# A four-layer graph network on one core: a node pass with longer lags, an edge pass with four transpose buffers and a reordered VectorE

## The reference

```
ft = (feat @ W).reshape(n, 8, 32)
e = leaky_relu(einsum(ft, attn_l)[src] + einsum(ft, attn_r)[dst])
ex = exp(e - segment_max(e, dst)[dst]);  alpha = ex / segment_sum(ex, dst)[dst]
x = layernorm(x + elu(segment_sum(ft[src] * alpha, dst)))
h = (x @ W3.T).reshape(n, 4, 64)          # start of the fourth layer
```

## Time and profile before

| | us |
|---|---|
| median of 3 runs (lowest, highest) | 5583.04 (5579.09, 5586.88) |
| the profiled execution, its own time | 5618.38 |
| its span, first to last instruction | 5616.6 |
| busy PE, DVE, ACT, POOL | 4466.3, 3371.4, 1907.7, 3767.0 |
| edge pass of layer two, first POOL instruction to the barrier | 3246.9 to 3890.6 |
| node pass, from there to its barrier | 3890.6 to 4580.8 |

### The profile page before, as it was taken

The page is one execution under the profiler, slowest core; times in us unless marked ns, Lnnn a source line. Parts: engine busy times, 40 slices in busy tenths (PEclk is TensorE's granted clock), DMA queues, the critical chain, the costliest instruction groups (busy, mean ns, idle before and its releaser), DMA issues. The chain is left out here.

```text
span 5616.6 us, 68003 instructions
## 1 busy us (share of the span) xinstructions
PE 4466.3 (80%) x17208; PEld 2963.8 (53%) x17208; DVE 3371.4 (60%) x9357; ACT 1907.7 (34%) x3319; POOL 3767.0 (67%) x3395
## 2 busy tenths in 40 slices
PE   2477669999999999999999967774777656656765
PEld 1255435556666666666666656664666533322222
DVE  1255456566666666666666547676555548945655
ACT  0011135532222222222222244453444420026765
POOL 7488644445777777777777767774555568856674
PEclk7688889999999999999999988886888978878887
DMA  9999899987744334433334255655777756658886
GB/s 378 307 202 207 193 279 365 361 310 275 260 136 133 128 127 132 134 132 127 123 131 132 99 181 200 217 212 176 259 264 261 264 189 226 240 172 282 309 310 218
DMA packets 530526, 1214.70 MB, mean 216 GB/s; under 512 B 172297, under 2 KB 267697, under 8 KB 530370
## 3 DMA queue, kind: packets, MB, share of 16 engines
q1 hardware_dynamic: 344392, 963.16, 48.4%
q0 software_dynamic: 147728, 214.04, 14.3%
q10 hardware_dynamic: 38250, 35.85, 2.0%
HBM read 623.69 MB, written 721.15 MB: 239 GB/s over the span
## 5 line engine op out<-in xcount | busy, mean ns | idle before, releaser
L1123 PE MATMUL psum<-W2b,arena 128*128 128x256 f32 x3136 | 725.2, 379 | 0.0
L840 DVE TENSOR_SCALAR arena<-arena 128x256 f32<-128x256 f32 x784 | 476.9, 669 | 388.2 <-POOL arena L835 383.4
L1104 PE MATMUL psum<-arena,W1b 128*128 128x512 f32 x1568 | 699.1, 599 | 0.0
L1123 PEld LDWEIGHTS psum<-W2b,arena 128*128 128x128 f32 x3136 | 573.1, 190 | 66.3 <-issue 0.5
L1946 POOL DMA_INDIRECT hd_d<-arena,FL x392 | 382.2, 975 | 306.6 <-DVE arena L1992 185.2
L618 PE MATMUL psum<-arena,half 128*128 128x324 f32 x980 | 355.2, 528 | 284.0 <-ACT arena L409 156.6
L2092 POOL DMA_INDIRECT arena<-fin_d,FL x392 | 427.3, 1090 | 184.6 <-issue 118.0
L1012 ACT ACTIVATE arena<-psum,hbias 128x512 f32<-128x512 f32 x392 | 270.0, 689 | 804.2 <-PE psum L1104 794.7
L1104 PEld LDWEIGHTS psum<-arena,W1b 128*128 128x128 f32 x1568 | 289.8, 190 | 402.4 <-issue 402.4
L967 POOL DMA_INDIRECT xl_d<-arena,FL x392 | 389.0, 992 | 118.7 <-issue 116.4
L959 POOL DMA_INDIRECT xd_d<-arena,FL x360 | 378.6, 1052 | 99.5 <-issue 99.2
(11 more groups left out here) (291 smaller groups left out, 8926.4 us busy)
## 6 DMA issues: line engine op xcount, KB each, us to landing
arena<-in_x SPq DMA_DIRECT2D x194, 512.0 KB
x_d<-arena SPq DMA_DIRECT2D x194, 512.0 KB
tab<-zero SPq DMA_DIRECT2D x11, 5832.0 KB
arena<-x_d SPq DMA_DIRECT2D x105, 512.0 KB
h_d<-arena SPq DMA_DIRECT2D x97, 528.0 KB
arena<-h_d SPq DMA_DIRECT2D x97, 528.0 KB
h_d<-arena SPq DMA_DIRECT2D x98, 512.0 KB
arena<-h_d SPq DMA_DIRECT2D x98, 512.0 KB
```

The lines of the kernel that those rows point to most:

```text
L840: v.tensor_scalar(y[:, j, :], r[:, j, :], self.mv[:, j, 0:1], self.rs[:, j:j + 1], ALU.subtract, ALU.mult).then_inc(self.s["y"], 1)
L1104: last = pe.matmul(psum[:, HB[c], :], W1b[:, f, c * P:(c + 1) * P], x1T[:, f, :], start=False, stop=(f == FH - 1))
L1123: last = pe.matmul(outB(j), hid[:, c, j * P:(j + 1) * P], W2b[:, c, :], start=(c == 0), stop=(c == KH - 1))
```

## The change

In the edge pass there are 4 PSUM banks and 4 `xT` buffers for transposes in place of 2 (and 4 banks in place of 6 for products). PE transposes 3 chunks ahead of its products in place of 1, ACT copies out 2 ahead in place of 1. DVE's turn g becomes logits(g), finish(g-2), shares(g), chain(g) in one piece. POOL scatters 23 chunks behind in place of 25. The elu stands one chunk earlier in ACT's order, and in the join the last `finish` stands in DVE's list behind the first four operations of the join. In the node pass to_rows stands 6 turns behind in place of 4 and the store of hs 4 turns behind in place of 2; xT has 4 buffers, so that evac(k) waits for mm(k-4); and the stores of hs count on semaphores of their own (`gd`), so that normed waits for stores of y alone and to_rows for those of hs alone. What other phases count on is adapted.

```diff
@@ edge_pass2
-            F0, NF = 2, 6
+            NT, NF = 4, 4
...
-            LAG = 25
+            LAG = 23
-                return F0 + c % NF
+                return NT + c % NF
...
-                    wait(pe, r["ev"], c - 1)
+                    wait(pe, r["ev"], c - NT + 1)
-                tr(0)
+                for c in range(NT - 1):
+                    tr(c)
                 for c in range(C):
-                    if c + 1 < C:
-                        tr(c + 1)
+                    if c + NT - 1 < C:
+                        tr(c + NT - 1)
                     mm(c)
-                    wait(act, r["mm"], c - 1)
+                    wait(act, r["mm"], c - NT + 1)
-                    if c + 1 < C:
-                        ev(c + 1)
+                    if c + NT - 2 < C:
+                        ev(c + NT - 2)
                     projected(c)
-                    elif j == 5 and g >= 2:
+                    elif j == 4 and g >= 2:
                         elu(g - 2)
-                logits(0)
-                shares(0)
                 for g in range(NE):
-                    if g + 1 < NE:
-                        logits(g + 1)
-                    chain(g, 0, 3)
-                    if g > 0:
-                        finish(g - 1)
-                    if g + 1 < NE:
-                        shares(g + 1)
-                    chain(g, 3, JE)
+                    logits(g)
+                    if g > 1:
+                        finish(g - 2)
+                    shares(g)
+                    chain(g, 0, JE)
-                finish(NE - 1)
-                join.vector(v)
+                finish(NE - 2)
+                join.vector(v, lambda: finish(NE - 1))
@@ node_pass
-            xT = take([2, FH, STEP])
+            xT = take([NB, FH, STEP])
+            HLAG = 6
-            def out_wait(eng, k):
-                wait(eng, n_w[b], 32 * k.turn(NB) + W4[b])
+            def rows_out(eng, k):
+                wait(eng, n_w[b], 16 * k.turn(NB) + W4[b])
+            def heads_out(eng, k):
+                wait(eng, gd[b], 16 * k.turn(NB) + 16 * (NE // 2))
-                    if not (k.known() and k.s < 2):
-                        store_h(k.plus(-2))
+                    if not (k.known() and k.s < HLAG - 2):
+                        store_h(k.plus(2 - HLAG))
-                    wait(act, r["mm"], 2 * (k.s - 1))
+                    wait(act, r["mm"], 2 * (k.s - NB + 1))
-                    if not (k.known() and k.s < 4):
-                        to_rows(k.plus(-4))
+                    if not (k.known() and k.s < HLAG):
+                        to_rows(k.plus(-HLAG))
```

More of the change, by code:

```diff
@@ L1164, in gnn_program @@
         W4 = [W2[b] + 16 * THIRDS[b] for b in range(NB)]
-        W5 = [W4[b] + 32 * USES[b] for b in range(NB)]
+        W5 = [W4[b] + 16 * USES[b] for b in range(NB)]
         W6 = [W5[b] + 16 * THIRDS[b] for b in range(NB)]
@@ L1221, in scalar, with vector @@
                 act.activation(self.wf, self.df, ACT.Exp).then_inc(r["f0"], 1)
-            def vector(self, v):
+            def vector(self, v, meanwhile=None):
                 r, T, H, F0, MC = once, self.T, self.H, self.F0, self.MC
@@ L1233, in vector @@
                 v.tensor_copy(newrow, self.endrow).then_inc(r["fr"], 1)
+                if meanwhile:
+                    meanwhile()
                 n0 = 9 * (T - 1)
@@ L1269, in edge_pass2 @@
             xl = take([2, JE, D])
-            xT = take([2, 4, P])
+            xT = take([NT, 4, P])
             ft = take([2, JE, TW])
@@ L1383, in tr @@
                         pe.wait_ge(r["head"], 16)
-                    wait(pe, r["ev"], c - 1)
+                    wait(pe, r["ev"], c - NT + 1)
                     for i, a in enumerate((xs[:, c % RING, :], xd[:, (c // JE) % 2, c % JE, :])):
                         for f in range(FH):
-                            done = pe.transpose(psum[:, c % 2, (2 * i + f) * P:(2 * i + f + 1) * P], a[:, f * P:(f + 1) * P], ident[:, :])
+                            done = pe.transpose(psum[:, c % NT, (2 * i + f) * P:(2 * i + f + 1) * P], a[:, f * P:(f + 1) * P], ident[:, :])
                     done.then_inc(r["tr"], 1)
@@ L1394, in mm @@
                     for f in range(FH):
-                        pe.matmul(o[:, 0:D + H], xT[:, c % 2, f, :], Wg[L][:, f, 0:D + H], start=(f == 0), stop=(f == FH - 1))
+                        pe.matmul(o[:, 0:D + H], xT[:, c % NT, f, :], Wg[L][:, f, 0:D + H], start=(f == 0), stop=(f == FH - 1))
                     for f in range(FH):
-                        done = pe.matmul(o[:, D + H:D + 2 * H], xT[:, c % 2, 2 + f, :], Wg[L][:, f, D + H:D + 2 * H], start=(f == 0), stop=(f == FH - 1))
+                        done = pe.matmul(o[:, D + H:D + 2 * H], xT[:, c % NT, 2 + f, :], Wg[L][:, f, D + H:D + 2 * H], start=(f == 0), stop=(f == FH - 1))
                     done.then_inc(r["mm"], 1)
-                tr(0)
+                for c in range(NT - 1):
+                    tr(c)
                 for c in range(C):
-                    if c + 1 < C:
-                        tr(c + 1)
+                    if c + NT - 1 < C:
+                        tr(c + NT - 1)
                     mm(c)
@@ L1409, in ev @@
                     act.wait_ge(r["tr"], c + 1)
-                    wait(act, r["mm"], c - 1)
-                    act.activation(xT[:, c % 2, :, :], psum[:, c % 2, :].rearrange("p (i n) -> p i n", n=P), ACT.Copy).then_inc(r["ev"], 1)
+                    wait(act, r["mm"], c - NT + 1)
+                    act.activation(xT[:, c % NT, :, :], psum[:, c % NT, :].rearrange("p (i n) -> p i n", n=P), ACT.Copy).then_inc(r["ev"], 1)
                 def projected(c):
@@ L1439, in g_scalar @@
                 act.wait_ge(r["zero"], 5)
-                ev(0)
+                for c in range(NT - 2):
+                    ev(c)
                 for c in range(C):
-                    if c + 1 < C:
-                        ev(c + 1)
+                    if c + NT - 2 < C:
+                        ev(c + NT - 2)
                     projected(c)
@@ L1873, in body @@
                         rows(k.plus(NH))
-                    if not (k.known() and k.s < 2):
-                        store_h(k.plus(-2))
+                    if not (k.known() and k.s < HLAG - 2):
+                        store_h(k.plus(2 - HLAG))
                 run_beats(sp, NS, body, NH, peel=NH, tail=NH)
-                for s in range(NS - 2, NS):
+                for s in range(NS + 2 - HLAG, NS):
                     store_h(beat(s, NH))
@@ L1898, in body @@
                         for f in range(FH):
-                            last = pe.matmul(psum[:, 2 + j, 0:HW], xT[:, k.slot(2), f, j * P:(j + 1) * P], Wg[3][:, f, :], start=(f == 0), stop=(f == FH - 1))
+                            last = pe.matmul(psum[:, 2 + j, 0:HW], xT[:, k.slot(NB), f, j * P:(j + 1) * P], Wg[3][:, f, :], start=(f == 0), stop=(f == FH - 1))
                         if j % 2 == 1:
@@ L1922, in evac @@
                     act.wait_ge(r["tr"], k.s + 1)
-                    wait(act, r["mm"], 2 * (k.s - 1))
+                    wait(act, r["mm"], 2 * (k.s - NB + 1))
                     for f in range(FH):
-                        act.activation(xT[:, k.slot(2), f, :], psum[:, f, :], ACT.Copy).then_inc(r["xT"], 1)
+                        act.activation(xT[:, k.slot(NB), f, :], psum[:, f, :], ACT.Copy).then_inc(r["xT"], 1)
                 def body(k):
@@ L2000, in body @@
                         newton(k.plus(-2))
-                    if not (k.known() and k.s < 4):
-                        to_rows(k.plus(-4))
+                    if not (k.known() and k.s < HLAG):
+                        to_rows(k.plus(-HLAG))
                 run_beats(v, NS, body, NH, peel=NH)
                 newton(beat(NS - 2, NH))
-                for s in range(NS - 4, NS):
+                for s in range(NS - HLAG, NS):
                     to_rows(beat(s, NH))
@@ L2030, in last_pass @@
             n_g = gs + sc
-            H0 = [16 * USES[b] + 16 * EIGHTHS[NB + b] for b in range(NB)] + [16 * (NE // 2) * n for n in (2, 2, 1, 1)]
+            H0 = [16 * USES[b] + 16 * EIGHTHS[NB + b] for b in range(NB)] + [16 * (NE // 2) * n + 16 * USES[b] for b, n in enumerate((2, 2, 1, 1))]
             X0 = [16 * USES[b] + 16 * EIGHTHS[b] for b in range(NB)]
```

10 lines of the change are left out of this document (6 added, 4 removed).

## The result

The changed kernel takes 5686.7 us (median of 4 runs, 5679.0 to 5694.9), the kernel before 5585.0 beside it: ratio 1.0182 (95% 1.0162 to 1.0201). It is 1.8% slower, +102 us. I had forecast 5602, +19, with 5652 as the upper end of the range.

A forecast was written before the change was run, and what follows sets the result against it. POOL, 95% occupied, was taken to bound the edge pass and a loop of waits the node pass. Node pass +57 and edge pass -38 gave +19 us, 5602 against the median of 5583.0; range 5514 to 5652.

The forecast's parts named there:

- The loop: Node pass after: copy waits for transpose, behind a product waiting for late to_rows; guess and newton follow; 12.9 us a pair.
- 12.9 + 1.74 = 14.6 ... I take 14.8: Node pass: full-clock loop plus today's clock loss per pair, with a longer loss in one pair of six.
- the forecast's +57: Node pass total: 46 pairs from 13.7 to 14.8 us, +51, plus +6 for the two more turns of lag.
- 5.88 us at to_rows: Node pass before: DVE's wait there, holding up statistics and newton, within a loop summing to the 13.70 us period.
- Rival 2: Node pass: longer clock loss in every pair, 15.9 us; +69 us, total 5652; chance 0.13.
- Rivals 1 and 4: 1: clock holds wholly or partly, pair 12.9 to 13.9, chance 0.22. 4: edge pass gives nothing, 5640, chance 0.15.
- Rival 3: Node pass: backward loop doesn't bind; POOL's 10.2 us or DMA is next, say 11.5 a pair; 5450; chance 0.08.
- Edge pass -38: Edge pass: middle -19, start -5 and end -16 sum to -40 us, taken as -38.
- Start: Edge pass: first scatter comes 2 gathers earlier, without most of the 6.85 us wait: -5 us, bounds 0 and -8.
- Start and middle together: Edge pass: start -5, and -19 of POOL's 20.6 us of mid-pass waits for PE's transposes.
- The end: Edge pass: POOL's waits of 12.61 and 4.41 us for finish go: -16 us, bounds -4 and -16.
- finish, join, semaphores at nothing: Both passes: later finish without mid-pass POOL waits, last finish inside the join, and split semaphores, each costed at nothing.

The follow-up runs named there:

- n7_ahead6: Changed kernel (lag 6) with PE's node-pass transposes two steps ahead of its products in place of one: ratio 0.9957 to the kernel before, pair 13.6 us.
- n15_one6: Changed kernel (lag 6) with one scatter of heads a step in place of four: ratio 1.0057 to the kernel before, node pass 739.2 us, pair 14.9.
- n13_fill44: Changed kernel with 44 added identity transposes into a free bank ahead of every second product: ratio 1.0211 to the kernel before, pair 16.4 us.
- n1_lag4: Changed kernel with to_rows back at 4 turns behind, all else kept: ratio 0.9963 to the kernel before, node pass 692.6 us, pair 13.8.
- n3_lag5: Changed kernel with to_rows 5 turns behind in place of 6: ratio 0.9945 to the kernel before, pair 13.7 us.
- n9_few5: Changed kernel at lag 5 with POOL's scatters of heads writing 32 rows in place of 128: ratio 0.9967 to the kernel before, pair 13.7 us.
- n12_half5: Changed kernel at lag 5 with each node-pass product over half its inputs: ratio 0.9906 to the kernel before, pair 13.0 us.

## Why the prediction was wrong

- **The loop**: right. Product behind to_rows, transpose behind product, copy, guess, newton; every arrow is in the waits, and one product less in it (n7_ahead6) or a smaller lag takes the loss away.
- **"12.9 + 1.74 = 14.6 ... I take 14.8"**: the failed step. The sum has only the loop and the clock in it. Without three of four scatters the pair is 14.9 (14.1 to 15.9) and the node pass 739, where the forecast's +57 makes 747. What it lacks is a term, put at nothing without a word: PE's results come late to ACT and DVE while POOL issues scatters. It is 16.05 - 14.90 = 1.15 us a pair, 46 x 1.15 = +53 of the 54 that separate +57 from +111 (the whole pass is 62 us shorter in n15_one6). The 65.8 us by which the copies are late are of that size. How the 14.9 divides between the loop's 12.9 and the clock no run shows, as none with one scatter a step at lag 6 kept the clock up; the agreement is one of totals.
- **"5.88 us at to_rows" before**: I took the 13.70 us of the earlier trace rows apart into six waits and they closed, so I looked no further. Steps from start to start around one pair always add up to its period, so this could not fail. The late counts were in that trace already: 8 copies, and 46 of the 196 halves of to_rows, start more than 1 us late, and 42 of the 46 stand 1.6 to 1.8 us behind the end of a scatter. The pair of the earlier trace rows is one of them:

```profile
4217.08 0.97 POOL L1946 DMA_INDIRECT hd_d<-arena,FL  x1 [0.30 <-issue]
4221.82 0.97 POOL L1946 DMA_INDIRECT hd_d<-arena,FL  x1 [3.77 <-DVE arena L1992]
```

  A row of eight scatters ends at 4218.05, to_rows starts at 4219.72, 1.67 later, though the first half of its product ends at 4218.27 by the record. The next row starts 2.10 behind it, and a row of eight takes 9.91: 1.67 + 2.10 + 9.91 = 13.68, a second sum that closes. The product's second half ends at 4220.05, so that to_rows could have been done only 0.3 us sooner: the two are nearly a tie there. Lag 5 at 13.7, with quite other waits, speaks for the scatters, though it has 25 rows of four beside 31 of eight. Whether they bound lag 4 by themselves no run shows, as the one with few scatters had lag 5.
- **Rival 2** named 15.9 a pair, nearly the measured number, for a wrong reason: n13_fill44 keeps the clock at full speed and the pair is 16.4. Its total of 5652 is still 35 us short of the measured one: 17 of them are the edge pass. Rivals 1 and 4 (a pair at 12.9 to 13.9, an edge pass that gives nothing) did not come.
- **Rival 3** (POOL next at 10.2, no pair above 11.5) ranked POOL by its busy time, and so missed what POOL does to others.
- **Edge pass -38**: -25 in the profile, -21 by n1_lag4. Start: the first scatter comes at 3309.07, not 3317.54. With the same number of DMAs ahead of it that is 4.7 us earlier, for -5, but by luck: the wait of 6.85 us did not go, POOL stands 6.62 there, now for DVE's `finish`. Half of the 4.7 are shorter waits for PE before it, half DMAs that happened to run shorter. Start and middle together: the last copy (3833.86 in the earlier trace rows) is at 3813.46, -20.6 with the passes' starts set equal, for -24. The end failed: from that copy to the fetch of old rows it was 3878.49 - 3833.86 = 44.6 us and is 3854.65 - 3813.46 = 41.2, -3.4 for -16. POOL's two waits there did go, as forecast, but the copies had moved ahead of POOL, which then has its scatters still to issue one by one. The bound of -4 was the right end. Over the pass 34 us of waits went and 10 came back as longer DMAs and their issue, which I had costed at 0.6. The lines after, from the timelines of POOL and DVE:

```profile
3309.07 1.01 POOL L1355 DMA_INDIRECT r_d<-arena,IDX  x1 [6.62 <-DVE arena L1543]
...
3813.46 0.20 DVE L1490 COPY arena<-arena 128x56 f32<-128x56 f32 x1
...
3854.65 0.99 POOL L1193 DMA_INDIRECT arena<-agg_d,slotg  x1 [0.30 <-issue]
```

- **finish, join, semaphores at nothing**: right. The end has no wait of POOL for finish, and edge pass 3 is 390.2 after 387.8.

## What to carry to other kernels

Price a lag by the backward path as well: with one set of banks, an evacuation moved two turns later moves the next product, the next transpose and all that queues behind them. A row of a slow engine's DMAs is not only that engine's time: where a consumer starts microseconds after its producer's recorded end, look at what POOL does in between, and test the number of its DMAs, not their bytes. A sum of waits that closes exactly is no proof, as it closes by construction; check each consumer's start against the recorded end of what it waits for. Another lag that gives the same period is a reason to look for a second bound. Of the versions run that compute all, a lag of 5 with the new edge pass is the fastest, 0.9945 (0.9929 to 0.9962); those with lag 4, with transposes two ahead, and with half of the edge pass's change alone are not told apart from it.

## What was not expected of the hardware

- While POOL issues indirect DMAs back to back, PE's results reach ACT mostly 2 to 6 us after their recorded end, up to 10.8 in n3_lag5, 12.3 in n9_few5 and 12.7 in n12_half5, mostly 1 to 2 us behind the end of a scatter. With one scatter a step in place of four: never above 0.13. The Trainium skill ("Trainium Architecture — The Big Picture", section "What this means for kernel authors") says that the engines are independent processors, and that among the engines' own accesses to SBUF only the port pair of VectorE and GpSimd contends. Neither leads one to expect this; here TensorE's consumers are held up with POOL's scatters, and the measurement decides. By which path they are held up no run shows. Whether PE itself stands or only its signals are late stays open. For the first: transposes without a wait stop for 1.7 us in n13_fill44. For the second: in n3_lag5 PE is idle from 4112.7 by the record, and the granted clock is 1.00 up to 4117, 0.65 in the microsecond after and 0.50 from 4118 on, as behind an idle PE, while ACT still waits for its transposes. Their semaphore is counted at 4118.38 and that of the two halves of the product behind them at 4118.47 and 4118.56, in a burst, where the recorded ends are 4107.71, 4109.49 and 4112.67.
- A scatter of 32 rows costs POOL 1.17 us, one of 128 rows 1.28: the price is nearly all by the piece.
- In the changed kernel the granted clock fell to 0.50 (4211 to 4217) behind PE's idle time of 5.7 us in the pair shown, as in the earlier trace rows, and n13_fill44 kept it at 1.00; yet at lag 6 the full clock bought nothing, because the row of scatters ended last.
